# LoRA columns transposed by a product with the identity, one chunk earlier, and fewer waits on TensorE

## The chip, the cores and the metric

The kernel runs on one core of a Trainium2 chip. The metric is the device time of one execution in microseconds (us). The kernel before takes 803.95 us, the median of three runs (803.92 to 804.58). The engines are called PE (TensorE), DVE (VectorE), ACT (ScalarE), POOL (GpSimd) and SP (SyncE, which issues the DMAs here). They run side by side, each through its own list of instructions in order, and tell each other by semaphores when something is ready.

## The reference

For each of 64 items x is 128 by 1024 (channels by positions). A first layer adds x multiplied by a 128 by 128 matrix that the item picks from a table of 200; a second adds a dense 1024 by 1024 layer and a LoRA branch of rank 16, whose adapter (one of 8) and scale the item picks too:

```python
def _L0_cond_ref(x, conditions, weights):
    w = weights[conditions]
    return jnp.einsum('bct,bcd->bdt', x, w)

def _L1_cond_ref(x, W, A, Bm, scalings, adapter_idx):
    H = jnp.einsum('btd,od->bto', x, W)
    xa = jnp.einsum('btd,brd->btr', x, A[adapter_idx])
    delta = jnp.einsum('btr,bor->bto', xa, Bm[adapter_idx])
    return H + delta * scalings[adapter_idx][:, None, None]

x = x + _L0_cond_ref(x, itok_B_1_198, L0_cond_weights)
x = x + _L1_cond_ref(x, L1_cond_W, ..., itok_B_0_6)
```

## The kernel before

Both layers are linear, so the kernel applies the second one first: z = x (I + W^T) plus the LoRA branch, then the output is (I + w)^T z. Every float32 operand is split into a high and a low part (names that end in `_hi` and `_lo`, type fp32r), and a product is three TensorE products: high by high, high by low, low by high.

Two items form a pair. The dense layer of a pair is done by Winograd's form of Strassen's scheme: item 0 and item 1 and the two halves of the 1024 inputs give sums s1 to s4, and seven products with blocks of the weights (called J1 to J7) give the four blocks of the result. A product with one block runs over four chunks of 128 inputs (k = 0 to 3). The function `riding` makes it as two products of 256 columns, of which the second is up to 32 columns wider so that the LoRA-A columns ride along; `plain` makes it as one product of 512 columns (for the PSUM bank `delta`) or two of 256 (for `beta`).

One call of `step(i, j)` on every engine does the dense layer of one pair and the per-item matrix products of the pair before it. The call is written out for the first steps and the last two; a loop on every engine holds two calls for the rest. There are 31 steps with a dense layer (the first pair is done by code of its own ahead of them) and a last call that has only the per-item matrices. In one step PE works in this order, fixed by the code: J2 into `beta`, J1 into `alpha`, J4 into `beta`; `condition(…, 0)` (six products of 512 columns for the earlier item of the pair before); J6 into `beta`; J3 into `delta` with the transpose of the LoRA columns inside it, behind chunk k = 2; the LoRA products into `delta` and `alpha`; `condition(…, 1)` for the later item; J7 into `beta` (line 880) and its LoRA products; J5 into `delta` and its LoRA product.

The LoRA branch runs through three engines. DVE gathers the LoRA columns of the pair in `xa_cols` (the last of them at line 718, which signals `xa_ready`); PE transposes that 128 by 128 tile into the PSUM bank `xaT_ps` (line 925); ACT makes three masked copies of it, `g_second`, `g_first`, `g_both`, in this order (lines 508 to 510), each of which raises `g_ready` by one; PE multiplies them with the LoRA-B rows in `b_stack` (function `lora`, lines 891 and 894). Before, PE waits for the first copy ahead of line 891, for the second ahead of line 894, and for the third at the end of the step.

Behind the first LoRA product, `delta` goes on: ACT copies it out (`d1_sb`, line 512), DVE adds `beta` to it (line 726, signals `c22_summed`), and PE may then write over `beta` at line 880.

`condition` waits, for each half h of an item's 1024 columns, for that half of z: `z11_ready` then `z12_ready` for the earlier item, `z21_ready` then `z22_ready` for the later one. `z12_ready` is signalled by DVE line 670 at the start of the following step, after line 662 and ACT line 472; it hangs on the last product of the step before it.

Of the kernel before, what the change touches and what calls it, by code (L numbers as in the profile page):

```python
# [7 lines left out]
def cond_resid_kernel(nc, xT, cond_idx, adapter_idx, cond_w, wB, lora_a, lora_b, scalings, out):  # L8
# [31 lines left out]
    with ExitStack() as ctx:  # L40
# [32 lines left out]
        ident = sb("ident", [P, P], f32)  # L73
        mask = sb("mask", [P, 3], f32)
# [44 lines left out]
        mask_ready = sem("mask_ready")  # L119
        zeros_ready = sem("zeros_ready")  # L120
# [103 lines left out]
        def done(i, j, d, per=1):  # L224

            return (i * 2 + (j + d)) * per
# [399 lines left out]
        def _(dve):  # L626
# [197 lines left out]
            rest_of(M12, wr_lo[:, :, J6 * RS:J6 * RS + H], w_c, wr_hi[:, :, J6 * RS:J6 * RS + H])  # L824
            dve.wait_ge(w_lo_ready, M12)
# [34 lines left out]
        def _(pe):  # L860
# [11 lines left out]
            def plain(bank, left_hi, left_lo, o, opens, between=None):  # L872

                for k in range(KH):
                    for left, right in ((left_hi, wn_hi), (left_hi, wn_lo), (left_lo, wn_hi)):
                        begins = opens and k == 0 and left is left_hi and right is wn_hi
                        ends = k == KH - 1 and left is left_lo
                        if bank is beta:
                            for h in range(2):
                                last = nc.tensor.matmul(bank[:, h, 0:Q], left[:, k, :], right[:, o, k, h * Q:(h + 1) * Q],  # L880
                                                        start=begins, stop=ends, skip_group_check=not opens)
                        else:
                            last = nc.tensor.matmul(bank[:, :], left[:, k, :], right[:, o, k, :],  # L883
                                                    start=begins, stop=ends, skip_group_check=not opens)
                    if between and k == 2:
                        between()
                return last
# [10 lines left out]
            def condition(i, j, n):  # L898

                pe.wait_ge(c_ready, loaded(i, j, -1))  # L900
                for h in range(2):
                    if n:
                        pe.wait_ge(z22_ready if h else z21_ready, done(i, j, -1))
                    else:
                        pe.wait_ge(z12_ready if h else z11_ready, done(i, j, -1))
# [10 lines left out]
            def step(i, j):  # L916
                first = exists(i, j, 0) and not exists(i, j, -1)

                def transpose_xa():
                    pe.wait_ge(xa_ready, done(i, j, 0, 2))  # L920
                    if first:
                        pe.wait_ge(first_out, 2)
                    else:
                        pe.wait_ge(g_ready, done(i, j, -1, 3))
                    nc.tensor.transpose(xaT_ps[:, 0:P], xa_cols[:, :], ident[:, :]).then_inc(xaT_done, 1)  # L925
# [22 lines left out]
                if exists(i, j, 0):  # L948
# [6 lines left out]
                    if not first:  # L955
                        pe.wait_ge(c12_summed, done(i, j, -1))
                    plain(delta, s1_hi, s1_lo, J3, True, transpose_xa)
                    pe.wait_ge(b_ready, loaded(i, j, 0))
                    pe.wait_ge(g_ready, done(i, j, -1, 3) + 1)
                    lora(delta, g_second, H).then_inc(d1_done, 1)  # L960
                    pe.wait_ge(g_ready, done(i, j, -1, 3) + 2)
# [3 lines left out]
                if exists(i, j, 0):  # L965
                    if first:
                        pe.wait_ge(w_lo_ready, MT4)
                    pe.wait_ge(c22_summed, done(i, j, 0))
                    pe.wait_ge(a22_ready, done(i, j, 0))
                    plain(beta, a22_hi, a22_lo, J7, False)  # L970
                    lora(beta, g_second, 0).then_inc(beta_done, 1)
                    pe.wait_ge(d1_ready, done(i, j, 0))
                    pe.wait_ge(s4_ready, done(i, j, 0))
                    plain(delta, s4_hi, s4_lo, J5, False)
                    pe.wait_ge(g_ready, done(i, j, 0, 3))
# [23 lines left out]
            def transpose_first_xa():  # L999
                pe.wait_ge(first_xa, 2)  # L1000
                nc.tensor.transpose(xaT_ps[:, 0:P], xa_cols[:, :], ident[:, :]).then_inc(first_xaT, 1)
# [82 lines left out]
```

## Time and profile before

| | value |
|---|---|
| median of three runs | 803.95 us |
| the profiled execution's own time | 804.07 us |
| its span | 802.3 us |
| PE busy | 780.4 us, 97% of the span |
| DVE, ACT, POOL busy | 66%, 48%, 18% |
| share of PE in the chain that ended last | 92% |
| granted PE clock, mean | 0.994 |

The span is what the profile sees from the first instruction to the last; the 1.8 us between it and the execution's own time lie outside every engine. A row of a timeline has the start in us from the span's start, the duration, the engine, the line in the code, the operation, the tile written and the tiles read, and in brackets how long the engine had been idle and who ended it. PEld is the loading of a product's left operand into the array, which overlaps the product before. Products overlap too: one of 512 columns is shown as 0.39 us long, but the next starts 0.23 us after it. So the distance from one start to the next is what a product costs, and a duration above the usual one means that it started to stream late.

### The profile page before, as it was taken

How to read it: one execution, taken by the hardware profiler on the slowest of the kernel's cores; microseconds unless marked ns; L12 is line 12 of the kernel's file. 1: busy time of each engine (PE TensorE's matmuls, PEld its weight loads, DVE VectorE, ACT ScalarE, POOL GpSimd, SP SyncE). 2: the span in 40 equal slices, each digit the busy share in tenths (PEclk: the TensorE clock that was granted, in tenths of full speed). 3: DMA queues.
4: the chain of work that ended last, by engine and by line, in shares of the span. 5: the costliest groups of instructions: out<-in, count | busy, mean ns of one | idle time of the engine just before them, and what ended most of it. 6: DMA issues, size and time to landing. Idle time of an engine off the chain costs nothing.

```text
span 802.3 us, 16191 instructions
## 1 busy us (share of the span) xinstructions
PE 780.4 (97%) x5216; PEld 716.3 (89%) x5216; DVE 530.1 (66%) x923; ACT 382.8 (48%) x719; POOL 146.8 (18%) x302
## 2 busy tenths in 40 slices
PE   5979999999999999999999999999999999999996
PEld 5878999999999999999999999999999999999994
DVE  5886776666776666776666776666776666776653
ACT  5554445444544444545444445444445444444432
POOL 3612222012222012222012222012222012222000
PEclk9989999999999999999999999999999999999999
DMA  8332333322333322333322333322333322333111
GB/s 291 119 103 83 122 138 132 113 95 91 122 137 131 111 95 91 122 137 131 111 96 90 122 137 131 111 94 91 122 137 131 111 96 89 122 137 131 53 60 78
DMA packets 45190, 92.54 MB, mean 115 GB/s; under 512 B 7540, under 2 KB 23924, under 8 KB 45172
## 3 DMA queue, kind: packets, MB, share of 16 engines
q1 hardware_dynamic: 44738, 92.17, 32.2%
q8 instruction: 10, 0.16, 0.1%
q10 hardware_dynamic: 434, 0.14, 0.1%
q14 instruction: 8, 0.07, 0.0%
HBM read 58.72 MB, written 33.55 MB: 115 GB/s over the span
## 4 chain that ended last, share of the span: by engine, by line
PE 92%; DVE 3%; DMA 2%; POOL 1%; issue 1%; SPq 0%; ACT 0%; ACTq 0%; POOLq 0%; DVEq 0%
PE beta L867 34%; PE delta L883 21%; PE beta L880 11%; PE alpha L867 11%; PE o_ps L912 4%; PE o_ps L913 3%; PE o_ps L914 3%; PE delta L891 2%; DMA a_now<-lora_a 1%; PE alpha L894 1%; PE beta L894 1%; DVE wn_lo L775 1%; DVE wr_lo L775 1%; PE xaT_ps L925 0%; DMA out<-o_sb 0%
## 5 line engine op out<-in xcount | busy, mean ns | idle before, releaser
L384 POOL TENSOR_TENSOR wr_lo<-a_ride,wr_hi 128x192 fp32r<-128x192 f32 x31 | 18.7, 602 | 578.6 <-ACT wr_hi L464 578.6
L867 PE MATMUL beta<-wr_hi,s_hi 128*128 128x256 f32 x496 | 102.4, 288 | 4.7 <-DVE xa_part L679 4.1
L867 PE MATMUL beta<-wr_hi,s_lo 128*128 128x256 f32 x496 | 102.1, 287 | 0.0
L867 PE MATMUL beta<-wr_lo,s_hi 128*128 128x256 f32 x496 | 101.9, 287 | 0.0
L883 PE MATMUL delta<-wn_hi,s_hi 128*128 128x512 f32 x248 | 99.9, 403 | 0.0
L883 PE MATMUL delta<-wn_hi,s_lo 128*128 128x512 f32 x248 | 97.2, 392 | 0.0
L883 PE MATMUL delta<-wn_lo,s_hi 128*128 128x512 f32 x248 | 96.9, 391 | 0.0
L752 DVE COPY o_sb<-o_ps 128x512 f32<-128x512 f32 x62 | 42.5, 685 | 80.5 <-PE o_ps L914 77.7
L867 PEld LDWEIGHTS beta<-wr_hi,s_hi 128*128 128x128 f32 x496 | 80.7, 191 | 7.8 <-issue 4.2
L867 PEld LDWEIGHTS beta<-wr_lo,s_hi 128*128 128x128 f32 x496 | 78.9, 191 | 0.0
L867 PEld LDWEIGHTS beta<-wr_hi,s_lo 128*128 128x128 f32 x496 | 78.6, 191 | 0.0
L495 ACT ACTIVATE v_sb<-beta 128x512 f32<-128x512 f32 x31 | 18.6, 600 | 120.3 <-PE beta L867 120.3
L373 POOL TENSOR_TENSOR a_ride<-a_now,s_now 128x64 f32<-128x64 f32 x128 | 65.8, 544 | 26.3 <-DMA a_now<-lora_a 21.7
L508 ACT ACTIVATE g_second<-xaT_ps,mask 128x128 fp32r<-128x128 f32 x31 | 11.5, 370 | 96.1 <-PE xaT_ps L925 96.1
L883 PEld LDWEIGHTS delta<-wn_hi,s_lo 128*128 128x128 f32 x248 | 46.6, 188 | 10.5
L883 PEld LDWEIGHTS delta<-wn_hi,s_hi 128*128 128x128 f32 x248 | 46.5, 188 | 9.1
L880 PE MATMUL beta<-wn_hi,a_hi 128*128 128x256 f32 x248 | 51.2, 288 | 1.2 <-issue 1.2
L883 PEld LDWEIGHTS delta<-wn_lo,s_hi 128*128 128x128 f32 x248 | 46.7, 188 | 6.2
L867 PE MATMUL beta<-wr_hi,x_hi 128*128 128x256 f32 x248 | 51.2, 288 | 0.0
L867 PE MATMUL beta<-wr_hi,x_lo 128*128 128x256 f32 x248 | 51.1, 287 | 0.0
L867 PE MATMUL beta<-wr_lo,x_hi 128*128 128x256 f32 x248 | 50.9, 286 | 0.0
L867 PE MATMUL alpha<-wr_hi,x_lo 128*128 128x256 f32 x248 | 50.5, 285 | 0.0
(215 smaller groups left out, 1942.0 us busy)
## 6 DMA issues: line engine op xcount, KB each, us to landing
out<-o_sb SPq DMA_DIRECT2D x62, 512.0 KB, 2.7
x_even<-xT SPq DMA_DIRECT2D x32, 512.0 KB, 4.1
x_odd<-xT SPq DMA_DIRECT2D x30, 512.0 KB, 4.0
b_raw<-lora_b SPq DMA_DIRECT2D x192, 64.0 KB, 2.1
c_raw<-cond_w SPq DMA_DIRECT2D x64, 64.0 KB, 1.7
a_now<-lora_a SPq DMA_DIRECT2D x62, 64.0 KB, 2.2
w_raw<-wB SPq DMA_DIRECT2D x4, 512.0 KB, 8.2
x_even<-xT SPq DMA_DIRECT2D x4, 256.0 KB, 6.4
```

What stands on the lines that cost most here:

```text
L373: nc.gpsimd.tensor_tensor(a_ride[:, :, slot, :], a_now[:, n, k:k + KH, :], s_now[:, n:n + 1].unsqueeze(2).to_broadcast([P, KH, R]), ALU.mu ...
L384: nc.gpsimd.tensor_tensor(ride_of(wr_lo, J1, J2), a_ride[:, :, 0:3, :], ride_of(wr_hi, J1, J2), ALU.subtract).then_inc(ride_ready, 1)
L495: nc.scalar.activation(as_halves(v_sb[:, :]), halves(beta), ACT.Copy).then_inc(v_ready, 1)
L752: nc.vector.tensor_copy(o_sb[:, H:T], o_ps[1][:, :]).then_inc(o_right, 1)
L775: nc.vector.tensor_tensor(two(to, half), two(raw, half), two(hi, half), ALU.subtract)\
L867: last = nc.tensor.matmul(bank[:, h, 0:hi - lo], left[:, chunk + k, :], right[:, k, lo:hi], start=opens and k == 0 and left is left_hi and ...
L880: last = nc.tensor.matmul(bank[:, h, 0:Q], left[:, k, :], right[:, o, k, h * Q:(h + 1) * Q], start=begins, stop=ends, skip_group_check=not ...
L883: last = nc.tensor.matmul(bank[:, :], left[:, k, :], right[:, o, k, :], start=begins, stop=ends, skip_group_check=not opens)
L891: return nc.tensor.matmul(bank[:, :], g[:, :], b_stack[:, cols:cols + H], start=False, stop=True, skip_group_check=True)
L912: nc.tensor.matmul(bank, c_hi[:, n, :], hi, start=True, stop=False)
L913: nc.tensor.matmul(bank, c_hi[:, n, :], lo, start=False, stop=False)
L914: return nc.tensor.matmul(bank, c_lo[:, n, :], hi, start=False, stop=True)
```

## The change

PE's transpose instruction, with a float32 identity, becomes an ordinary product of `xa_cols`, read as fp32r, with an fp32r identity. DVE makes that identity once, by a copy in the opening. The product is called behind chunk k = 1 of J3, not k = 2; in the opening, `first_right` still calls its own behind k = 2. Of PE's waits in a step, ten go: among them the two on the first halves of z (both halves now wait for the second half's signal), and the three on the copies of the transposed columns become one, for all three of them, ahead of the first LoRA product. The wait for `s4_ready` moves ahead of J7.

```diff
@@ DVE, opening @@
             rest_of(M12, wr_lo[:, :, J6 * RS:J6 * RS + H], w_c, wr_hi[:, :, J6 * RS:J6 * RS + H])
+            nc.vector.tensor_copy(ident_r[:, :], ident[:, :]).then_inc(ident_r_ready, 1)
@@ plain @@
-                    if between and k == 2:
+                    if between and k == 1:
                         between()
@@ condition @@
-                pe.wait_ge(c_ready, loaded(i, j, -1))
+                pe.wait_ge(z22_ready if n else z12_ready, done(i, j, -1))
                 for h in range(2):
-                    if n:
-                        pe.wait_ge(z22_ready if h else z21_ready, done(i, j, -1))
-                    else:
-                        pe.wait_ge(z12_ready if h else z11_ready, done(i, j, -1))
@@ step: transpose_xa @@
                     if first:
                         pe.wait_ge(first_out, 2)
-                    else:
-                        pe.wait_ge(g_ready, done(i, j, -1, 3))
-                    nc.tensor.transpose(xaT_ps[:, 0:P], xa_cols[:, :], ident[:, :]).then_inc(xaT_done, 1)
+                    nc.tensor.matmul(xaT_ps[:, 0:P], xa_cols[:, :].bitcast(f32r), ident_r[:, :], start=True, stop=True)\
+                        .then_inc(xaT_done, 1)
@@ step @@
-                    if not first:
-                        pe.wait_ge(c12_summed, done(i, j, -1))
                     plain(delta, s1_hi, s1_lo, J3, True, transpose_xa)
                     pe.wait_ge(b_ready, loaded(i, j, 0))
-                    pe.wait_ge(g_ready, done(i, j, -1, 3) + 1)
+                    pe.wait_ge(g_ready, done(i, j, 0, 3))
                     lora(delta, g_second, H).then_inc(d1_done, 1)
-                    pe.wait_ge(g_ready, done(i, j, -1, 3) + 2)
                     lora(alpha, g_first, 0).then_inc(alpha_done, 1)
...
+                    pe.wait_ge(s4_ready, done(i, j, 0))
                     pe.wait_ge(c22_summed, done(i, j, 0))
-                    pe.wait_ge(a22_ready, done(i, j, 0))
                     plain(beta, a22_hi, a22_lo, J7, False)
                     lora(beta, g_second, 0).then_inc(beta_done, 1)
-                    pe.wait_ge(d1_ready, done(i, j, 0))
-                    pe.wait_ge(s4_ready, done(i, j, 0))
                     plain(delta, s4_hi, s4_lo, J5, False)
-                    pe.wait_ge(g_ready, done(i, j, 0, 3))
                     lora(delta, g_both, H).then_inc(delta_done, 1)
```

The first place is on PE, in the loop: the end of J3 with the transpose and the first LoRA products. The names are those above; REGISTER_ALU rows only work out the loop's wait values. Before, from the last product of chunk k = 2 on:

```order
L883 MATMUL delta<-wn_hi,s1_lo 128x512
L920 REGISTER_ALU
L924 REGISTER_ALU [waits xa_ready]
L925 MATMUL xaT_ps<-ident,xa_cols 128x128 [waits g_ready]
L883 MATMUL delta<-wn_hi,s1_hi 128x512
L883 MATMUL delta<-wn_lo,s1_hi 128x512
L883 MATMUL delta<-wn_hi,s1_lo 128x512
L959 REGISTER_ALU [waits b_ready]
L891 MATMUL delta<-b_stack,g_second 128x512 [waits g_ready]
L961 REGISTER_ALU
L894 MATMUL alpha<-b_stack,g_first 128x256 [waits g_ready]
```

The same place in the change, from the transposing product on:

```order
L923 MATMUL xaT_ps<-ident_r,xa_cols 128x128 [waits xa_ready]
L886 MATMUL delta<-wn_hi,s1_hi 128x512
L886 MATMUL delta<-wn_lo,s1_hi 128x512
L886 MATMUL delta<-wn_hi,s1_lo 128x512
L886 MATMUL delta<-wn_hi,s1_hi 128x512
L886 MATMUL delta<-wn_lo,s1_hi 128x512
L886 MATMUL delta<-wn_hi,s1_lo 128x512
L956 REGISTER_ALU [waits b_ready]
L894 MATMUL delta<-b_stack,g_second 128x512 [waits g_ready]
L897 MATMUL alpha<-b_stack,g_first 128x256 x2
```

Three products stood between the transpose and the first LoRA product, and now six do; the LoRA product for `alpha` no longer waits.

The second place is the end of PE's program: the last LoRA product and the per-item products of the last pair's earlier item (`z_hi0` and `z_lo0` are its z, `o_ps0` and `o_ps1` the PSUM banks of its two output halves). Before:

```order
L891 MATMUL delta<-b_stack,g_both 128x512 [waits g_ready]
L912 MATMUL o_ps0<-z_hi0,c_hi 128x512 [waits o_left,z11_ready,c_ready]
L913 MATMUL o_ps0<-z_lo0,c_hi 128x512
L914 MATMUL o_ps0<-z_hi0,c_lo 128x512
L912 MATMUL o_ps1<-z_hi0,c_hi 128x512 [waits o_right,z12_ready]
```

And in the change:

```order
L894 MATMUL delta<-b_stack,g_both 128x512
L912 MATMUL o_ps0<-z_hi0,c_hi 128x512 [waits o_left,z12_ready]
L913 MATMUL o_ps0<-z_lo0,c_hi 128x512
L914 MATMUL o_ps0<-z_hi0,c_lo 128x512
L912 MATMUL o_ps1<-z_hi0,c_hi 128x512 [waits o_right]
```

The wait for the second half of z has moved from the second group of three products to the first.

## Rows read from the trace of the kernel before

**Rows 1.** Waits: engine, line, awaited; total us, times, longest.
```profile
PEld beta L880 <- DVE d_sb L726: 6.1, 30, 0.2
PEld delta L891 <- ACT g_second L508: 5.2, 26, 0.2
PE beta L867 <- DVE xa_part L679: 4.1, 1, 4.1
```
**Rows 2.** Timeline of one step in the loop, J3 to J7, all engines.
```profile
323.81 0.17 DVE L718 TENSOR_TENSOR xa_cols<-beta,xa_cols 128x16 fp32r<-128x16 f32 x1
...
324.54 0.39 PE L883 MATMUL delta<-wn_hi,s_lo 128*128 128x512 f32 x1
...
325.22 0.39 PE L883 MATMUL delta<-wn_hi,s_lo 128*128 128x512 f32 x1
...
325.45 0.27 PE L925 MATMUL xaT_ps<-ident,xa_cols 128*128 128x128 f32 x1
325.45 0.19 PEld L883 LDWEIGHTS delta<-wn_hi,s_hi 128*128 128x128 f32 x1
...
325.56 0.19 PEld L883 LDWEIGHTS delta<-wn_lo,s_hi 128*128 128x128 f32 x1
...
325.75 0.37 ACT L508 ACTIVATE g_second<-xaT_ps,mask 128x128 fp32r<-128x128 f32 x1 [3.11 <-PE xaT_ps L925]
...
326.02 0.40 PE L883 MATMUL delta<-wn_hi,s_lo 128*128 128x512 f32 x1
...
326.17 0.19 PEld L891 LDWEIGHTS delta<-b_stack,g_second 128*128 128x128 f32 x1 [0.20 <-ACT g_second L508]
...
326.27 0.37 ACT L510 ACTIVATE g_both<-xaT_ps,mask 128x128 fp32r<-128x128 f32 x1
...
327.35 0.69 DVE L726 TENSOR_TENSOR d_sb<-beta,d_sb 128x512 f32<-128x512 f32 x1 [1.02 <-ACT d_sb L512]
...
328.09 0.30 PEld L880 LDWEIGHTS beta<-wn_hi,a_hi 128*128 128x128 f32 x2 [0.20 <-DVE d_sb L726]
```
**Rows 3.** Line 891's products: count, duration min/median/max ns, first and last start.
```profile
L891 PE MATMUL delta<-b_stack,g_second x31: 424/424/475, 61.3 to 783.6; 128*128 128x512 f32 x31
L891 PE MATMUL delta<-b_stack,g_both x31: 394/394/394, 69.2 to 791.4; 128*128 128x512 f32 x31
```
**Rows 4.** The page's groups: J3 and J5 products, count, busy us, mean ns.
```profile
L883 PE MATMUL delta<-wn_lo,s_hi 128*128 128x512 f32 x248 | 96.9, 391 | 0.0
```
**Rows 5.** Timeline of the second step, which is written out.
```profile
84.68 0.27 PE L925 MATMUL xaT_ps<-ident,xa_cols 128*128 128x128 f32 x1
...
85.47 0.19 PEld L891 LDWEIGHTS delta<-b_stack,g_second 128*128 128x128 f32 x1 [0.26 <-issue]
```
**Rows 6.** Timeline of the first step, J3 to J7.
```profile
59.61 0.39 PE L883 MATMUL delta<-wn_hi,s_lo 128*128 128x512 f32 x1
...
60.09 0.17 DVE L718 TENSOR_TENSOR xa_cols<-beta,xa_cols 128x16 fp32r<-128x16 f32 x1
...
61.31 0.19 PEld L891 LDWEIGHTS delta<-b_stack,g_second 128*128 128x128 f32 x1 [0.26 <-issue]
...
61.85 0.60 ACT L512 ACTIVATE d_sb<-delta 128x512 f32<-128x512 f32 x1
...
62.52 0.68 DVE L726 TENSOR_TENSOR d_sb<-beta,d_sb 128x512 f32<-128x512 f32 x1
...
63.27 0.30 PEld L880 LDWEIGHTS beta<-wn_hi,a_hi 128*128 128x128 f32 x2 [1.43 <-issue]
```
**Rows 7.** Timeline of the end of the kernel.
```profile
791.66 0.39 PE L912 MATMUL o_ps<-z_hi,c_hi 128*128 128x512 f32 x1
...
793.99 0.50 PE L912 MATMUL o_ps<-z_hi,c_hi 128*128 128x512 f32 x1 [1.48 <-DVE z_lo L670]
...
794.79 0.40 PE L912 MATMUL o_ps<-z_hi,c_hi 128*128 128x512 f32 x1
```
**Rows 8.** Timeline of DVE in the opening.
```profile
25.40 1.34 DVE L775 TENSOR_TENSOR wn_lo<-x_odd,wn_hi 128x1024 fp32r<-128x1024 f32 x1 [3.69 <-ACT wn_hi L541]
```

More of the change, by code:

```diff
@@ L73, in cond_resid_kernel @@
         ident = sb("ident", [P, P], f32)
+        ident_r = sb("ident_r", [P, P], f32r)
         mask = sb("mask", [P, 3], f32)
@@ L119, in cond_resid_kernel @@
         mask_ready = sem("mask_ready")
+        ident_r_ready = sem("ident_r_ready")
         zeros_ready = sem("zeros_ready")
@@ L999, in transpose_first_xa @@
             def transpose_first_xa():
+                pe.wait_ge(ident_r_ready, 1)
                 pe.wait_ge(first_xa, 2)
-                nc.tensor.transpose(xaT_ps[:, 0:P], xa_cols[:, :], ident[:, :]).then_inc(first_xaT, 1)
+                nc.tensor.matmul(xaT_ps[:, 0:P], xa_cols[:, :].bitcast(f32r), ident_r[:, :], start=True, stop=True)\
+                    .then_inc(first_xaT, 1)
             pe.wait_ge(ident_ready, 1)
```

## Prediction, on record before the changed kernel ran

> **What bounds the kernel now.** I read the table of waits first, since PE is busy 97% of the span. The reader is to see that TensorE (PE) hardly waits: the one long wait of its products is 4.1 us, once, in the opening [rows 1]. Only two weight loads wait once in every step: the one of the first LoRA product (line 891) for ACT's copy `g_second`, 26 times in the loop, and the one of line 880 for DVE's sum `c22_summed`, 30 times, up to 0.2 us each [rows 1]. The timeline of one step in the loop shows the rest: products of 512 columns start every 0.227 us (324.54 to 325.22 is three of them), and a step takes 24.08 us, from the transposes at 84.68 and 325.45, ten steps apart [rows 2, 5]. So a part of the change counts only if it changes PE's own work, or one of those two waits, or the opening or the end, where PE is not the bound.
>
> **The transposing product.** What the transpose costs PE: from 325.22 to 326.02 stand three products of 512 columns and the transpose, 0.80 us; less 3 x 0.227 it is 0.12 us. The weight loads say why: the load of the product behind it starts at 325.45, the next at 325.56 [rows 2]. A load takes 0.11 us of the array's input, and a product of 128 columns is too short to hide it; its place costs 0.11 us whatever it does in it. The trace has no ordinary product of 128 columns. From below: the next load still takes 0.11 us, so it gains at most the 0.01 us between 0.12 and 0.11, 0.3 us over 31 steps. From above: if it takes as long as one of four times the columns, its place is 0.227 us, 0.117 us more, 3.6 us over 31 steps. I take 0: the fp32r products here stream 512 columns in 0.227 us, so 128 would be over within the 0.11 us of the load, and that row is the nearest.
>
> The profile shows no drawback of an ordinary product in these rows. The Trainium skill ("Perfetto Trace Analysis", section "Transposes") says the contrary: a transpose should be a transpose instruction and not a standard matmul, because it skips the arithmetic; and "FP8 and Floating Point Precision", section "TensorE Precision Notes", gives true FP32 four passes through the array. By the rows the sum is 803.6 us; with four passes it would be 807.2 us. No row of before decides whether the new product counts as full or reduced precision.
>
> **The wait for the copies.** Before, the load of line 891 could have started with the product ahead of it, at 326.02, but starts at 326.17, 0.05 us after `g_second` is done (325.75 + 0.37) [rows 2]. That it is 0.15 us late costs less than that, since a load fills only 0.11 of a 0.227 us place: the product lasts 424 ns where an on-time one lasts 391, so it costs 0.033 us [rows 3, 4]. In the steps written out the load comes 0.79 us behind the transpose (85.47 - 84.68), not 0.72 (326.17 - 325.45), and the product lasts up to 475 ns: 0.084 us [rows 2, 3, 5]. About 0.12 us of lateness is free.
> Now PE waits for all three copies, and `g_both` ends 0.52 us after `g_second` (326.64 against 326.12). But the transpose comes three products, 0.68 us, earlier. Counted from its start: the third copy ends at 1.19 (326.64 - 325.45), its load could go at 1.24. PE meanwhile has 0.11 for the transpose and six products; the load of line 891 may start with the sixth, at 0.11 + 5 x 0.227 = 1.25. On time, with another 0.12 us free. `xa_cols` is early enough: DVE is done at 323.98, the transpose's load would start at 324.54 [rows 2]. So the cost goes: 26 x 0.033 + 4 x 0.084 = 1.2 us gained.
>
> What is late next is line 880. Its load waits for product 891, then ACT, then DVE line 726 (327.35 + 0.69 = 328.04, load at 328.09) [rows 2]. This chain starts with product 891 and moves with it, so the 1.2 us stay; but whatever PE saves between 891 and 880 (the dropped wait at 894, the merged ones of the per-item products) it waits longer at 880. I count it at nothing.
>
> **The other waits.** Ten waits go in a step. Apart from those for the copies, none shows in the table of waits [rows 1]. A product whose wait was long fulfilled lasts 394 ns (`g_both` at line 891), one without a wait 391 in the mean [rows 3, 4]: 3 ns, and I allow 5, if it is the wait. From below, nine waits at 5 ns over 31 steps are 1.4 us gained; from above 0, since most of these instructions keep another wait. Outside the stretch from 891 to 880 two instructions lose their only waits (J5's first product and its LoRA product): 2 x 5 ns x 31 = 0.3 us gained. The wait for `s4_ready`, now ahead of J7, costs nothing: DVE makes `s4_lo` ahead of `xa_cols`, done at 323.98, 4.1 us before line 880 [rows 2]. Behind it stand J7 and J5, which would cost their full delay if DVE were late; it is not.
>
> **The identity's copy.** One DVE copy of 128x128 in the opening. It delays DVE by at most the 0.7 us of a 512-column operation of its own; DVE then idles 3.69 us before 25.40 [rows 8], which hides it. Bounds 0 and 0.7; I take 0. The opening's own transpose stays behind k = 2.
>
> **The first step.** Here DVE is late. The transpose's load would now go at 59.61, but `xa_cols` is ready at 60.26 (60.09 + 0.17), load 60.31 [rows 6]. Before, three products stood behind it and now six do. The load, 0.11 later the transpose streams, 0.11 for it, six products (1.36) and 891 streams at 61.90. Before it streamed 0.11 behind its load at 61.31, at 61.42. So it comes 0.48 us later, and with it ACT, DVE line 726 and the load of 880 (63.27), which already waited 1.43 us for them. DVE began its sum at 62.52, 0.07 us behind the end of ACT's copy (61.85 + 0.60), so it was itself a little late then; I take 0.03 off and the loss is 0.45 us. Nothing gives it back.
>
> **The end.** Before, the first half of the last pair's earlier item was multiplied at 791.66, while DVE and ACT still made the second half of z, and the second half at 793.99, after 1.48 us of idling [rows 7]. Now both wait for the second half. The first group of three takes the place at 793.99, the second comes three products, 0.69 us, later, and with it the copy and the store of the output, which end the kernel. Loss 0.7 us: from below 0 if the store is held by something else, from above 0.8, the whole 793.99 to 794.79.
>
> **The sum** against the profiled execution's 804.07 us (span 802.3 and 1.8 outside it): -1.2 -0.3 +0.45 +0.7 + 0 = -0.35, or 803.7. The median of the runs is 0.1 lower, so I forecast 803.6 us: a change that works in the loop and is paid for at both ends.
>
> **Rivals.**
> Rival A, slower: the 128-column product is not done in 0.11 us but in four passes. Place: line 923 of the change, 31 times. For it: this product alone has fewer than 256 columns; every other fp32r product has 256 or more, so their pace proves nothing for it. Against: the weight loads of fp32r follow at 0.11 us, so nothing in the load is fourfold [rows 2]. It decides from the point where the product takes over 0.11 us; at 0.227 it costs 3.6 us: 807.2 us. The copies would still be in time, as PE's products move back with it.
> Rival B, the change doesn't do what it says: waiting for the last copy replaces waiting for the first. My account has the load just on time with 0.12 us free. If ACT starts or copies later than before by more than that, each further 0.05 us costs 31 x 0.05 = 1.6 us; at 0.1 us, 803.6 + 3.1 = 806.7 us. Against: ACT idled 3.11 us before the first copy [rows 2], so it starts when PE is done.
> Rival C, faster: waits cost PE's own list of instructions time that no row names as a wait. At 5 ns for all nine, and with the 0.01 us of the transpose's place, 1.4 + 0.3 instead of 0.3: 802.2 us. Against it the line 880 chain, which takes back about half.
>
> **How the numbers follow.** Forecast 0.60; A 0.27; B 0.05; C 0.08. What a measurement of this kernel can tell from no change is 0.2%, 1.6 us: below 802.3 counts as faster, above 805.6 as slower. Forecast within: 0.60. A and B slower: 0.32. C faster: 0.08. The forecast's own range is 802.8 to 804.6 (waits 1.4 instead of 0.3 below; the end and first step as priced, the gain at 891 half lost above). For 8 in 10 the range must reach to A, the only rival with weight: 802.6 to 807.4.
>
> **What would show it.** The distance from the product before the transpose to the second one behind it, less two places of 0.227: 0.11 to 0.12 if right, 0.22 or more for A; the shown duration of the transposing product near or under 0.27, or near the 0.39 of a 512-column one. The wait of 891 for ACT gone from the table and its products at 389 to 394 ns (B: still over 420). The wait at 880 grown, not gone. Steps in the loop about 0.03 to 0.05 us shorter than 24.08. PE idle of about 0.5 us ahead of the first step's transpose. At the end, PE idle for over 2 us and then six products in a row. The forecast is wrong if the step in the loop is longer than 24.08, or if it is shorter by more than 0.08.

## The result, and the profile after

The changed kernel takes 806.96 us, the median of six runs, against 803.86 us (803.0 to 804.58) of the kernel before. One of the six took 1116.8 us at a mean clock of 0.642; the median of the other five is 806.44 us (806.04 to 808.16), and the ratio leaves that one out. The ratio is 1.0037, 95% interval 1.0025 to 1.0048: slower by about 3 us. The forecast was 803.6 us and no measurable change; the time is inside the range of 802.6 to 807.4, near its upper end, but not for the reason (rival A) that put the end there.

The profiled execution took 806.44 us, with a span of 804.7 us against 802.3. Where the 2.4 us lie can be read from one product that every step has once and that nothing delays: the last LoRA product, `g_both`. The view of that tile, in the kernel after (duration min/median/max in ns, first and last start):

```profile
L512 ACT ACTIVATE g_both<-xaT_ps,mask x31: 368/368/369, 61.3 to 784.5; 128x128 fp32r<-128x128 f32 x31
L894 PE MATMUL delta<-b_stack,g_both x31: 392/394/395, 69.8 to 793.1; 128*128 128x512 f32 x31
```

Before, it ran from 69.2 to 791.4 [rows 3]. So up to the first one 0.6 us were lost, in the 30 steps between the first and the last 1.1 us (723.3 - 722.2), and behind the last 0.7 us (804.7 - 793.1 against 802.3 - 791.4). The ends were forecast at 0.45 and 0.7. The steps were forecast to gain 1.5.

The waits after (total us, times, longest), those that answer to [rows 1] and those of the two ends:

```profile
PE beta L870 <- DVE xa_part L681: 3.6, 1, 3.6
PE o_ps L912 <- DVE z_lo L672: 2.2, 1, 2.2
...
PE xaT_ps L923 <- DVE xa_cols L720: 0.3, 1, 0.3
...
PEld beta L883 <- issue: 9.8, 31, 1.4
```

The weight load's wait for ACT is gone. The one at J7 (line 883, before 880) is now 9.8 us in 31 times with one of 1.4 among them, so 8.4 in the 30 others, where it was 6.1. And its releaser is no longer "DVE d_sb" but "issue": the load itself waits for nothing that it carries. That word is the whole finding; what it hides is seen in the timeline of one step in the loop, kernel after, which answers to [rows 2]:

```profile
324.75 0.18 DVE L720 TENSOR_TENSOR xa_cols<-beta,xa_cols 128x16 fp32r<-128x16 f32 x1
...
325.48 0.40 PE L886 MATMUL delta<-wn_hi,s_lo 128*128 128x512 f32 x1
...
325.71 0.22 PE L923 MATMUL xaT_ps<-ident_r,xa_cols 128*128 128x128 f32 x1
325.71 0.19 PEld L886 LDWEIGHTS delta<-wn_hi,s_hi 128*128 128x128 f32 x1
325.77 0.45 PE L886 MATMUL delta<-wn_hi,s_hi 128*128 128x512 f32 x1
325.82 0.19 PEld L886 LDWEIGHTS delta<-wn_lo,s_hi 128*128 128x128 f32 x1
325.97 0.37 ACT L510 ACTIVATE g_second<-xaT_ps,mask 128x128 fp32r<-128x128 f32 x1 [2.39 <-PE xaT_ps L923]
...
326.05 0.39 PE L886 MATMUL delta<-wn_lo,s_hi 128*128 128x512 f32 x1
...
326.49 0.37 ACT L512 ACTIVATE g_both<-xaT_ps,mask 128x128 fp32r<-128x128 f32 x1
...
326.98 0.19 PEld L894 LDWEIGHTS delta<-b_stack,g_second 128*128 128x128 f32 x1
...
328.27 0.69 DVE L728 TENSOR_TENSOR d_sb<-beta,d_sb 128x512 f32<-128x512 f32 x1 [1.01 <-ACT d_sb L514]
...
329.08 0.30 PEld L883 LDWEIGHTS beta<-wn_hi,a_hi 128*128 128x128 f32 x2 [0.28 <-issue]
```

The product in place of the transpose does what the forecast said: it lasts 0.22 us, the next two weight loads stand 0.11 apart, and from the product ahead of it to the second behind it is 0.57 us, 0.12 more than two places of 0.227. All three copies are there (326.49 + 0.37 = 326.86) when the load of line 894 goes at 326.98. But at J7 the sum ends at 328.96 and the load goes at 329.08, 0.12 us behind it; before it was 0.05 us [rows 2]. To the nanosecond it is 116 against 52 in the median of the steps. The start of the first LoRA product recurs every 24.108 us in the mean of the loop's steps, 24.066 before. That is above the 24.08 us which the forecast named as the sign of being wrong.

Between the sum and the load stands an instruction that no row of these views shows, since it is not counted as busy. The trace has it: in the kernel after, a semaphore instruction of 51 ns on PE at 329.005, which waits for `c22_summed`, and the load behind it carries the wait for `s4_ready`. Before, the same kind of instruction waited for `a22_ready` and ran at 326.77, long ahead of time, and the load itself carried the wait for the sum. The program's order of PE's instructions tells it without a clock: before

```
L880 MATMUL beta<-wn_hi,a_hi 128x256 [waits a22_ready,c22_summed]
```

and after

```
L883 MATMUL beta<-wn_hi,a_hi 128x256 [waits c22_summed,s4_ready]
```

The name that stands last is the one on the load; it is the wait that the code writes first. The others stand on semaphore instructions in front of it.

The first step, kernel after, which answers to [rows 6]:

```profile
59.73 0.39 PE L886 MATMUL delta<-wn_hi,s_lo 128*128 128x512 f32 x1
...
60.18 0.17 DVE L720 TENSOR_TENSOR xa_cols<-beta,xa_cols 128x16 fp32r<-128x16 f32 x1
...
60.41 0.19 PEld L923 LDWEIGHTS xaT_ps<-ident_r,xa_cols 128*128 128x128 f32 x1 [0.71 <-DVE xa_cols L720]
...
61.79 0.19 PEld L894 LDWEIGHTS delta<-b_stack,g_second 128*128 128x128 f32 x1
...
63.88 0.30 PEld L883 LDWEIGHTS beta<-wn_hi,a_hi 128*128 128x128 f32 x2 [1.44 <-issue]
```

The load of line 894 goes 0.48 us later than that of line 891 did (61.79 against 61.31), and the load at J7 0.61 later (63.88 against 63.27). J3 itself starts 0.11 later here (58.58 against 58.47), so the step's own loss is 0.50 at J7, of which 0.05 is the semaphore instruction again: 0.45 us is the late `xa_cols`. The end, kernel after, which answers to [rows 7]:

```profile
795.66 0.50 PE L912 MATMUL o_ps<-z_hi,c_hi 128*128 128x512 f32 x1 [2.17 <-DVE z_lo L672]
...
796.46 0.39 PE L912 MATMUL o_ps<-z_hi,c_hi 128*128 128x512 f32 x1
```

PE idles 2.17 us instead of 1.48, 0.69 more, the three products that it did in that time before.

### The profile page after: what moved, and what is told of

Its sections match the earlier page's. It is cut to its first block, busy times and chain, and to the rows that moved or that the text cites. A ratio compares the mean times of both kernels' runs of the same rounds, so it can differ in the third digit from the quotient of the medians.

```text
span 804.7 us, 15936 instructions
## 1 busy us (share of the span) xinstructions
PE 780.7 (97%) x5216; PEld 718.8 (89%) x5216; DVE 530.4 (66%) x924; ACT 382.6 (48%) x719; POOL 147.0 (18%) x302
## 4 chain that ended last, share of the span: by engine, by line
PE 92%; DVE 4%; DMA 2%; POOL 1%; SPq 0%; issue 0%; ACT 0%; ACTq 0%; POOLq 0%; DVEq 0%
PE beta L870 34%; PE delta L886 21%; PE beta L883 12%; PE alpha L870 11%; PE o_ps L912 4%; PE o_ps L914 3%; PE o_ps L913 3%; PE delta L894 2%; DMA a_now<-lora_a 1%; DVE wn_lo L777 1%; PE beta L897 1%; PE alpha L897 1%; DVE wr_lo L777 1%; POOL a_ride L375 0%; DMA out<-o_sb 0%
## 5 line engine op out<-in xcount | busy, mean ns | idle before, releaser
L870 PE MATMUL beta<-wr_hi,x_lo 128*128 128x256 f32 x248 | 51.1, 288 | 0.0
L912 PE MATMUL o_ps<-z_hi,c_hi 128*128 128x512 f32 x124 | 48.9, 394 | 2.3 <-DVE z_lo L672 2.2
```

The source lines that it names most:

```text
L870: last = nc.tensor.matmul(bank[:, h, 0:hi - lo], left[:, chunk + k, :], right[:, k, lo:hi], start=opens and k == 0 and left is left_hi and ...
L912: nc.tensor.matmul(bank, c_hi[:, n, :], hi, start=True, stop=False)
```

## The experiments

Each kernel is told by its edit against the kernel before or after. The column "30 steps" is the time between the first and the last start of the `g_both` product; "step in the loop" is the mean distance between the first LoRA products of the loop's 26 steps; "sum to load" is the median from the end of DVE's sum to the weight load of J7; "end" is from the last `g_both` product to the end of the span. All four are worked out from the starts in each run's trace, to the nanosecond, and then rounded. Ratios are those of the run's own comparison with the kernel before.

| run | median us | ratio, 95% interval | 30 steps | step in the loop | sum to load | end |
|---|---|---|---|---|---|---|
| before | 803.86 | 1 | 722.2 | 24.066 | 52 ns | 10.9 |
| after | 806.96 | 1.0037 [1.0025, 1.0048] | 723.3 | 24.108 | 116 ns | 11.6 |
| e1 | 804.74 | 1.0007 [0.9999, 1.0016] | 721.6 | 24.053 | 52 ns | 11.6 |
| e2 | 805.76 | 1.0019 [1.001, 1.0027] | 724.0 | 24.125 | 114 ns | 10.9 |
| e3 | 806.89 | 1.0033 [1.0021, 1.0045] | 723.0 | 24.100 | 115 ns | 11.6 |
| e4 | 805.46 | 1.0016 [1.0007, 1.0024] | 723.3 | 24.111 | 114 ns | 10.9 |
| e5 | 803.92 | 1.0007 [0.9997, 1.0016] | 722.1 | 24.060 | 53 ns | 10.9 |
| e6 | 803.65 | 0.9996 [0.9987, 1.0005] | 721.6 | 24.053 | 53 ns | 10.9 |
| e7 | 804.43 | 1.0009 [1.0, 1.0018] | 721.5 | 24.046 | 53 ns | 11.9 |
| e8 | 803.47 | 0.9994 [0.9985, 1.0003] | 722.0 | 24.059 | 53 ns | 10.9 |
| e9 | 802.70 | 0.9981 [0.9972, 0.999] | 721.5 | 24.047 | 53 ns | 10.9 |
| e10 | 803.50 | 0.9989 [0.9979, 0.9998] | 721.3 | 24.037 | 52 ns | 10.9 |

Before and e8 are one and the same kernel, each profiled once, and differ by 0.2 us in 30 steps and by 0.007 us a step. A difference of that size between two other rows says nothing. Spans aren't compared as a whole either, since they contain the opening, which differs from profile to profile of one kernel (e8).

### e1: the changed kernel, the sum's wait on the load again

```diff
-                    pe.wait_ge(s4_ready, done(i, j, 0))
                     pe.wait_ge(c22_summed, done(i, j, 0))
+                    pe.wait_ge(s4_ready, done(i, j, 0))
                     plain(beta, a22_hi, a22_lo, J7, False)
```

> The changed kernel with the waits for c22_summed and s4_ready ahead of J7 in the other order, and nothing else. Theory 1 (the changed kernel puts the late semaphore, DVE's sum, on an instruction of its own, which runs 51 ns and only then lets the weight load of line 883 go; 116 ns from the sum's end to the load instead of 52): the load comes 52 ns behind the sum again, the step in the loop falls from 24.108 to about 24.043 us, the kernel is 31 x 0.065 = 2.0 us faster than the changed one, about 804.5 to 805. Theory 2 (the step grew because the product ahead of J7 or the per-item products wait for something else, or because fewer waits let PE run into DVE's and ACT's accesses): step stays at 24.10 to 24.11, no gain. Theory 3 (s4_ready is late, which the move of its wait exposed): no gain, and the load still waits, now for line 713.

Two lines change places, and the ratio falls from 1.0037 to 1.0007. The sum and the load in the loop, kernel e1:

```profile
327.80 0.69 DVE L728 TENSOR_TENSOR d_sb<-beta,d_sb 128x512 f32<-128x512 f32 x1 [1.01 <-ACT d_sb L514]
...
328.55 0.30 PEld L883 LDWEIGHTS beta<-wn_hi,a_hi 128*128 128x128 f32 x2 [0.22 <-DVE d_sb L728]
```

The load is 0.06 us behind the sum by these rounded rows, and its releaser has its name back. The 30 steps take 1.7 us less than in the kernel after (721.6, 723.3; 2.0 was expected): the price of the order of two waits. The ends are as after.

### e2: the kernel before, with only this order turned

```diff
-                    pe.wait_ge(c22_summed, done(i, j, 0))
                     pe.wait_ge(a22_ready, done(i, j, 0))
+                    pe.wait_ge(c22_summed, done(i, j, 0))
                     plain(beta, a22_hi, a22_lo, J7, False)
```

> The kernel before with only the order of the waits for c22_summed and a22_ready ahead of J7 swapped. Theory 1: the load of line 880 comes 116 ns behind the sum, not 52; step in the loop 24.067 + 0.064 = 24.131 us, 2.0 us slower than before. Theories 2 and 3: nothing changes, 24.067.

The waits of kernel e2's weight loads:

```profile
PEld beta L880 <- issue: 9.3, 31, 1.5
PEld delta L891 <- ACT g_second L508: 5.1, 26, 0.2
```

The same change of name, and 1.8 us more in 30 steps (724.0 against 722.2) in a kernel that has nothing else of the change. It is neither the merged waits nor `s4_ready`'s lateness: `a22_ready`, written ahead of the sum's wait, takes the load from it just as `s4_ready` does. e1 and e2 together show the cause from both sides.

### e3: the changed kernel, with the transpose instruction in the steps

```diff
-                    nc.tensor.matmul(xaT_ps[:, 0:P], xa_cols[:, :].bitcast(f32r), ident_r[:, :], start=True, stop=True)\
-                        .then_inc(xaT_done, 1)
+                    nc.tensor.transpose(xaT_ps[:, 0:P], xa_cols[:, :], ident[:, :]).then_inc(xaT_done, 1)
```

> The changed kernel with the transpose instruction again in the steps (still behind k = 1; the opening keeps the product). Theory 1 with the prediction's account of the weight loads (its place is set by the next load, 0.11 us, whichever it is): step in the loop within 0.010 us of 24.108, kernel within 0.3 us of the changed one. Rival A of the prediction (product in four passes): 3.6 us faster, step 23.99. The first copy starts 0.05 us later, which is covered.

30 steps 723.0 us against 723.3, ratio 1.0033 against 1.0037: no slower product to be found. In the changed kernel, whose copies are in time either way, it doesn't matter which of the two is used; the transpose is 0.008 us a step the better, hardly more than the 0.007 between before and e8.

### e4: the changed kernel, each half of z waited for by itself

```diff
-                pe.wait_ge(z22_ready if n else z12_ready, done(i, j, -1))
+                pe.wait_ge(c_ready, loaded(i, j, -1))
                 for h in range(2):
+                    if n:
+                        pe.wait_ge(z22_ready if h else z21_ready, done(i, j, -1))
+                    else:
+                        pe.wait_ge(z12_ready if h else z11_ready, done(i, j, -1))
```

> The changed kernel with the waits of the per-item products as they were before (c_ready, and each half of z by itself). The prediction's account of the end: PE multiplies the first half at the end while the second is made, the end is 0.7 us shorter, the step in the loop stays at 24.108 within 0.005, because the instructions that carry the waits run ahead of a weight load that is late anyhow. If removed waits do save PE time, the loop step is up to 0.05 us longer, and the kernel is up to 1.5 us slower less the 0.7.

The end, kernel e4:

```profile
793.58 0.39 PE L916 MATMUL o_ps<-z_hi,c_hi 128*128 128x512 f32 x1
...
795.91 0.50 PE L916 MATMUL o_ps<-z_hi,c_hi 128*128 128x512 f32 x1 [1.48 <-DVE z_lo L672]
```

The first group is back beside DVE's work, the idle time is 1.48 us as before, and the end takes 10.9 us, 0.7 less. The steps are untouched (24.111 against 24.108), so the wait for both halves costs nothing in them. The two ratios, 1.0016 and 1.0037, say 1.7 us where the profile says 0.7; with intervals of 0.7 to 0.9 us to each side, that is no contradiction, and the profile's row is the sharper one.

### e5: the kernel before, with the change's opening alone

```diff
+            nc.vector.tensor_copy(ident_r[:, :], ident[:, :]).then_inc(ident_r_ready, 1)
...
+                pe.wait_ge(ident_r_ready, 1)
                 pe.wait_ge(first_xa, 2)
-                nc.tensor.transpose(xaT_ps[:, 0:P], xa_cols[:, :], ident[:, :]).then_inc(first_xaT, 1)
+                nc.tensor.matmul(xaT_ps[:, 0:P], xa_cols[:, :].bitcast(f32r), ident_r[:, :], start=True, stop=True)\
+                    .then_inc(first_xaT, 1)
```

> The kernel before with only the opening's edits: the fp32r identity (tensor and DVE copy) and the opening's transpose as a product. The steps are as before, 24.067 us. Theory O1 (the 1.0 us by which DVE's copy of the LoRA part, the start of J4 in the first step, comes later in all four changed kernels, 49.9 to 50.1 against 48.7 to 48.9 us, is caused by these edits): DVE's copy at about 50.0, kernel 0.5 to 1.2 us slower than before. Theory O2 (it comes from the adapter load that landed late and a DVE and a POOL operation meeting at 36 us, which differs from run to run whatever the kernel): either time can come, and the kernel's median is that of before within 0.3 us.

### e8: the kernel before, unchanged, with a profile of its own

> The kernel before, unchanged, profiled once more. O1: DVE's copy of the LoRA part starts at 48.7 to 48.9 us again. O2: it may start anywhere between 48.7 and 50.1. Its median shows what this comparison takes for no change: within 0.3 us of the kernel before.

These two belong together. In the profile after, PE got its next work in the opening 1.0 us later than before (`xa_part` was done at 50.1 us against 49.0), which nothing in the forecast explained. Of that, 0.37 us are there when DVE starts its `x_lo` at 36 us, and 0.66 come behind it. That row, in four timelines:

The kernel before, in the profile that the forecast was read from:

```profile
35.65 1.21 DVE L633 TENSOR_TENSOR x_lo<-x_even,x_hi 128x1024 fp32r<-128x1024 f32 x1
```

The kernel after:

```profile
36.01 2.35 DVE L635 TENSOR_TENSOR x_lo<-x_even,x_hi 128x1024 fp32r<-128x1024 f32 x1
```

e8, which is the kernel before to the letter:

```profile
35.65 2.36 DVE L633 TENSOR_TENSOR x_lo<-x_even,x_hi 128x1024 fp32r<-128x1024 f32 x1
```

and e5, with the change's opening:

```profile
35.28 1.21 DVE L635 TENSOR_TENSOR x_lo<-x_even,x_hi 128x1024 fp32r<-128x1024 f32 x1
```

It goes either way in the unchanged kernel alone (1.21 and 2.36), so it doesn't take the change to turn it; the identity's copy costs nothing that these runs can see (e5's ratio is 1.0007, the interval holds 1). In all twelve profiles the operation is long in seven (after, e1, e3, e4, e6, e7, e8) and short in five (before, e2, e5, e9, e10): a leaning of the changed kernels towards the long one can't be excluded by so few. What meets there is told in the last section; what decides it stays open.

Little of the 1.0 us reaches the steps: J3 starts only 0.11 us later. From `xa_part` to J3's first product it is 9.43 us in the profile before, with the granted clock at 0.50 (1.2 GHz of 2.4) for the first 6.0 of them, and 8.51 us in the profile after, with 3.4 at 0.50.

### e6: e1, with both ends as they were

```diff
-                    if between and k == 1:
+                    if between and k == behind:
...
-                    plain(delta, s1_hi, s1_lo, J3, True, transpose_xa)
+                    plain(delta, s1_hi, s1_lo, J3, True, transpose_xa, 2 if first else 1)
...
+                last = n == 0 and not exists(i, j, 0)
+                if last:
+                    pe.wait_ge(c_ready, loaded(i, j, -1))
+                    pe.wait_ge(z11_ready, done(i, j, -1))
+                else:
+                    pe.wait_ge(z22_ready if n else z12_ready, done(i, j, -1))
...
+                    if h and last:
+                        pe.wait_ge(z12_ready, done(i, j, -1))
```

(In the first step the three copies are also waited for one by one again.)

> The changed kernel with three repairs: the sum's wait on the weight load; in the first step alone the product behind k = 2 with its waits as before; in the last call alone the two halves of z waited for one by one. Expected: step 24.053, first step 0.45 us and end 0.7 us better than in the first experiment, so 804.74 - 1.15 = 803.6 us: 0.4 us below before in the steps (30 x 0.013), less whatever the opening costs. If the account of the two ends is wrong, it stays at 804.7.

The first step, kernel e6:

```profile
59.09 0.19 PEld L930 LDWEIGHTS xaT_ps<-ident_r,xa_cols 128*128 128x128 f32 x1 [0.23 <-DVE xa_cols L720]
...
59.94 0.19 PEld L894 LDWEIGHTS delta<-b_stack,g_second 128*128 128x128 f32 x1 [0.21 <-issue]
```

From the transposing product's load to that of line 894 it is 0.85 us, against 1.38 in the kernel after (61.79 - 60.41). From the start of J3 to the load at J7 it is 4.99 us, against 5.25 in e1 and 4.79 in the kernel before: 0.26 of the 0.46 us are back. The other 0.2 are in the first row: the transposing product's load waits 0.23 us for `xa_cols` and goes 2.03 us behind J3's start, where it goes 1.84 behind it in the kernel before. In the opening of this profile the granted clock was at 0.50 only from 39.4 to 42.8 us, so PE came to J3 in 7.00 us from `xa_part` (9.43 before) and found DVE late. e7 and e9, which have the product behind k = 2 in every step and no such lateness of DVE, have 4.79 and 4.78. The end is 10.9 us again. Ratio 0.9996: with the sum's wait in its place and both ends mended, nothing is left of the loss, and nothing measurable of the gain.

### e7: e1, with the product back behind chunk k = 2 and the three copies waited for one by one

```diff
-                    if between and k == 1:
+                    if between and k == 2:
...
-                    pe.wait_ge(g_ready, done(i, j, 0, 3))
+                    pe.wait_ge(g_ready, done(i, j, -1, 3) + 1)
                     lora(delta, g_second, H).then_inc(d1_done, 1)
+                    pe.wait_ge(g_ready, done(i, j, -1, 3) + 2)
...
+                    pe.wait_ge(g_ready, done(i, j, 0, 3))
                     lora(delta, g_both, H).then_inc(delta_done, 1)
```

> The changed kernel with the sum's wait on the weight load (as in the first experiment), the product behind k = 2 again and the three waits for the copies as before; so what is left of the change in the loop are the product in place of the transpose and the other dropped waits. If the move and the merged wait bring the 0.013 us a step that the first experiment kept (24.053 against 24.067): step 24.067. If the dropped waits bring it: 24.05. The first step loses nothing: 0.45 us better than the first experiment there, the end still 0.7 us worse than before. Kernel about 0.1 us from the first experiment's, 804.6.

The line 894 product in kernel e7 (min/median/max):

```profile
L894 PE MATMUL delta<-b_stack,g_second x31: 396/397/437, 62.0 to 783.6; 128*128 128x512 f32 x31
```

Here the product stands where the transpose stood, and yet it is 397 ns, not 424. The move isn't needed for that. The step is 24.046 us, with the move 24.053, and the first step costs what it did before (4.79 us from J3 to the load at J7). The ratio is no better than e1's, 1.0009 against 1.0007, with intervals that leave room for the 0.4 us of the first step. The longer end (11.9) isn't the edit's: in this profile TensorE's granted clock was 0.50 (1.2 GHz of 2.4) from 795.03 to 798.44, at the end of the kernel:

```profile
780.00:790.00 10.00, 10.00 (x62) 1.00 0.21 86
795.10:798.30 3.20, 3.20 (x9) 0.50 0.23 95
```

(Columns: window in us, PE's busy time in all and of its products with their count, granted clock, DMA share, GB/s.) A place of 512 columns took 0.43 us in it, not 0.23. PE had been idle for 2.17 us until 793.92, as in e1, e3 and the kernel after, which also have both halves of z behind one wait there and kept the full clock.

### e10: the kernel before, with nothing but the product in place of the transpose (in the opening and in the steps)

```diff
-                    nc.tensor.transpose(xaT_ps[:, 0:P], xa_cols[:, :], ident[:, :]).then_inc(xaT_done, 1)
+                    nc.tensor.matmul(xaT_ps[:, 0:P], xa_cols[:, :].bitcast(f32r), ident_r[:, :], start=True, stop=True)\
+                        .then_inc(xaT_done, 1)
```

> The kernel before with nothing but the ordinary product with the fp32r identity in place of the transpose, in the opening and in every step; every wait and place as before. Theory P: what is left of the gain at the first LoRA products comes from the product, which is 0.05 us shorter than the transpose, so that the first copy starts 0.05 us earlier and line 891's load is on time: its products at 396 to 400 ns instead of 424, the wait for ACT nearly gone from the table, step 24.045 to 24.055 us. Theory W: it comes from the dropped waits: step 24.06 us as before, line 891's products still near 424 ns. Either way the time is within 0.6 us of the kernel before; a product in four passes would give over 3 us more.

The waits and the products of line 894, kernel e10:

```profile
PEld delta L894 <- issue: 1.0, 5, 0.2
```
```profile
L928 PE MATMUL xaT_ps<-ident_r,xa_cols x31: 220/220/220, 60.1 to 781.4; 128*128 128x128 f32 x31
L894 PE MATMUL delta<-b_stack,g_second x31: 398/398/438, 60.9 to 782.2; 128*128 128x512 f32 x31
```

Theory P holds. The 26 waits for ACT are gone without a wait or a place touched, the products take 398 ns instead of 422 (e5), and the step is 24.037 us against 24.060: 0.8 us in 30 steps (721.26 against 722.06). The product is 24 ns shorter and the step 23; 24.045 to 24.055 us were expected. This is most of the gain (0.033 us a step) that the forecast had put down to the earlier place and the merged wait.

### e9: what is worth keeping

e7 with the last call of e6 (its diff is the `last` part shown there), so that of the change only the product and the dropped waits are left.

> The change with four of its parts taken back: the sum's wait rides on the weight load of J7 again, the product stands behind chunk k = 2, the three copies are waited for one by one, and in the last call alone the two halves of z are waited for one by one. Left of the change are the ordinary product and the dropped waits. If the accounts of the loop and of both ends add up: step 24.047 us, first LoRA product of the first step at the place it has in the kernel before, from the last LoRA product to the end of the span 18.7 us; against the kernel before 31 x 0.013 = 0.4 us less, so 0.2 to 0.7 us less, a ratio of 0.9991 to 0.9998 (the opening's half clock can add or take 1 us in the profiled run). If the ends hold a cost that the runs so far do not show, it is level with the kernel before or above it.

Median 802.70 against 804.01 us, ratio 0.9981, 0.9972 to 0.999: 1.3 us faster than the kernel before in the same comparison, and by the two ratios over 4 us faster than the changed one. It is a little more than the 0.2 to 0.7 us expected; the profile gives 0.5 to 0.7 in the steps (721.5 against the 722.0 to 722.2 of e8 and before), the same first step (4.78 us) and the same end (10.9), so the rest is not located. e10, in the same comparison, has the better steps (24.037 against 24.047) and the worse median (803.5 against 802.7); the intervals overlap, so which of the two is the better is not settled. The steps show no gain of the dropped waits: with them gone a step takes 0.010 us more, little over the 0.007 between two profiles of one kernel.

## Why the prediction was wrong

**The step that failed** is in the paragraph on the other waits: "The wait for `s4_ready`, now ahead of J7, costs nothing". It asked whether DVE makes `s4_lo` early enough, and it does, by over 4 us. It did not ask on which instruction the wait sits. Written ahead of the wait for `c22_summed`, it took the load from it and pushed the sum's wait onto a semaphore instruction of its own, 64 ns more between the sum and the load, in every step, on the one wait of the loop that ends late each time. That is 1.7 us in 30 steps by e1 and 1.8 by e2. The forecast had read the right rows: the 0.05 us between the sum and the load stood in it, and it was taken to move along unchanged ("This chain starts with product 891 and moves with it"). The order of PE's instructions, which needs no run, shows the two waits changing places.

The rows of before held the same effect elsewhere. In the five steps that are written out, the wait for ACT's first copy is not on the load of line 891 but on a semaphore instruction of 51 ns ahead of it. There the load comes 113 to 114 ns behind the copy, in the loop 50 to 51, and the releaser of its idle time is "issue" [rows 5]. That is the product of 475 ns instead of 424 [rows 3], the 0.084 us that the forecast priced without asking where it came from.

**The gain at the first LoRA products** was forecast at 0.033 us a step and credited to the move. With the product alone, e10 has 0.023 a step. The 0.033 compared the late product with J3's products of 391 ns; a LoRA product that is on time lasts 396 to 398, so 0.026 to 0.028 were to be had. The size was nearly right; but the transpose's successor brings it by being 0.05 us shorter (270 to 220 ns), which starts ACT's copies 0.05 us earlier, enough for a load that was 0.15 late with 0.12 free. The forecast priced the product's place (0.11 us, right) and not its end, on which ACT waits. The move then bought the same gain a second time, and cost something: from J3's first product to the first LoRA product it is 2.886 us with it (e1), 2.876 without (e9), 2.870 before. That is why e1 gains only 0.013 us a step on the kernel before. In the first step the move costs 0.45 us besides.

**The dropped waits**, "0.3 us gained" with a bound of 1.4: no gain to be seen. e9 against e10 has 0.3 us in 30 steps the other way, a few ns more at products at the end of J3 and in J7; before and e8, the same kernel, differ by 0.2 us in the same manner. Whether it is an effect at all stays open. Rival C, which needed 1.4 us gained, falls with it.

**Put together**, in 30 steps, from e5 to the kernel after: product -0.80 (e10), dropped waits +0.26 (e9), move and merged wait +0.08 (e1), the sum's wait apart +1.65 (the kernel after against e1), in all +1.19, which is 723.25 - 722.06. The two terms in the middle are too small to be told from nothing. The forecast had -1.5.

**The first step** (+0.45) and **the end** (+0.7) came out as worked out: 0.45 at the load of J7 and 0.7. Where PE stands idle, each product taken out of its idle time is paid in full; that was the surest part of the reading. **Rival A**, with a chance of 0.27, is refuted by the 0.11 us between two loads, by the next product, which starts 0.06 us behind it (325.77 - 325.71; a quarter of the 0.227 us of 512 columns), and by e3: a 128-column fp32r product is not done in four passes here. The Trainium skill ("Perfetto Trace Analysis", section "Transposes") wants a transpose done by the transpose instruction; no run shows an advantage of it beyond 0.008 us a step (e3), and where ACT waits for the result, as in e10, the ordinary product is the better by 0.023. **Rival B** is refuted too: the last copy ended 0.12 us ahead of the load, which went on time. The kernel is slower, then, for a reason that none of the rivals named. That the time still lies inside the stated range is luck: the range was drawn that wide for rival A.

One row was misread without harm: besides the 4.1 us, PE's products wait 8.1 us once in the opening of the kernel before (`alpha`, line 982, for DVE's `wr_lo`).

## What to carry to other kernels

Where a weight load or product has several waits, only one rides on it in these kernels and the rest stand ahead on semaphore instructions; find out which, in the program's order, and let it be the one that is fulfilled last (here the one written first: 0.05 us behind the sum on the load, 0.12 us behind it apart). "issue" as the releaser of a wait that is known to end with another engine's work is the sign that it went the other way. And before a thing is moved earlier for a wait's sake, see what shortening it alone gives: the move was paid for where the pipeline fills, and a merged wait where it drains.

## What the runs showed of the hardware

- A semaphore instruction on PE that ends a late wait lasts 51 ns and puts the weight load 114 to 116 ns behind the event instead of 52, in each of the kernels after, e2, e3 and e4. When it is fulfilled early, as the one for `a22_ready` before, the weight load goes 52 ns behind its own event all the same. The Trainium skill ("Perfetto Trace Analysis", section "Identifying Dependency Chains") says that such instructions may be inserted where several engines are waited for; the trace agrees, and adds the price.
- One place of 128 columns doesn't end its cost with itself: the products of 512 behind it start every 228 to 236 ns in the kernel after, and every 227 only from the second half of `condition` on. The same is seen behind J6's products of 256 columns, where J3 starts with 237 and 236. With six such places ahead of the first LoRA product instead of three, e1 loses 16 ns there of the 29 that its timely load gains.
- DVE and POOL: in the opening, POOL's `w_raw` and DVE's `x_lo` start 10 to 17 ns apart. In the kernels before (first profile) and e5 DVE's operation took 1.21 us and POOL's 2.35 and 2.36; in the kernels after and e8 it was POOL's 1.29 and DVE's 2.35 and 2.36. The one that is held up ends 1.1 us behind the other. The Trainium skill ("SBUF — State Buffer", section "Who interferes with whom") describes a port pair that the two share under an exclusive lock, and says that the one that issues first gets it; the durations fit a lock, but the records don't show that order: POOL's began first in all four. Held up or not, DVE's work behind it is 0.66 us later or earlier.
- The granted clock fell to 0.50 (1.2 GHz of 2.4) in the opening, at a different time in each profile: 48.2 to 55.1 before, 51.1 to 54.5 after, 39.7 to 43.1 in e3. In e7 it fell twice in the opening and once more at 795.03, 1.1 us after 2.17 us of idling; e1, e3 and the kernel after idle as long there and keep the full clock to beyond 800 us. What decides when it falls isn't shown by these runs.
